# Attention's values in split passes for two heads at a time, and a new order of the linear attention's statements

## The reference

```python
x = x + L0_attn(layernorm(x))   # 16 query heads, 4 key/value heads of 128, causal softmax
x = x + L0_ffn(layernorm(x))    # 8 gated experts of 256, all computed, weighted per token by a router
x = x + L1_attn(layernorm(x))   # gated delta rule: 6 heads, short convolutions of 4 taps, gate, output projection
x = x + L1_ffn(layernorm(x))    # per sequence the 2 best of 6 gelu experts, chosen from the mean over tokens
```

```python
scores = q @ k.T ; attn = softmax(where(causal, scores, min)) ; out = attn @ v ; return out @ Wo.T + bo
```

## Time and profile before

| | us |
|---|---|
| runs | 1166.28, 1169.13, 1170.8 (median 1169.13) |
| profiled execution, its own time | 1162.17 |
| its span | 1160.4 |
| busy: TensorE, VectorE, ScalarE, GpSimd | 1098.4, 829.4, 628.2, 209.6 |
| mean granted clock of TensorE | 0.965 of full |

### The profile page before, as it was taken

One profiled execution on the slowest core, in us unless ns is written; L12 is line 12 of the kernel. 1 busy time (PEld: TensorE's weight loads), 2 busy tenths in 40 slices (PEclk: granted clock), 3 DMA queues, 4 the chain that ended last, 5 costly groups with the idle time before them and its releaser, 6 DMA issues. The chain is left out here.

```text
span 1160.4 us, 26495 instructions
## 1 busy us (share of the span) xinstructions
PE 1098.4 (95%) x9990; PEld 937.1 (81%) x9990; DVE 829.4 (71%) x2423; ACT 628.2 (54%) x1607; POOL 209.6 (18%) x246
## 2 busy tenths in 40 slices
PE   6999999999999998999999999959889999998898
PEld 4898899889988998788888889846667777777687
DVE  5777467656765785867776775798998798877454
ACT  5644444444544453544434443457877877766552
POOL 0422222222222221441000000031022102220110
PEclk9999999999999999999999999978899999997899
DMA  9200000000000000201000000011000001100323
GB/s 310 89 6 2 1 1 1 1 1 1 1 1 1 1 1 22 80 1 29 1 1 1 1 1 1 32 60 32 3 34 33 25 10 34 33 2 2 103 69 105
DMA packets 26701, 32.90 MB, mean 28 GB/s; under 512 B 4960, under 2 KB 21968, under 8 KB 26576
## 3 DMA queue, kind: packets, MB, share of 16 engines
q1 hardware_dynamic: 26576, 31.22, 8.6%
HBM read 29.04 MB, written 2.17 MB: 27 GB/s over the span
## 5 line engine op out<-in xcount | busy, mean ns | idle before, releaser
L333 DVE TENSOR_TENSOR a_ps<-a_ps,causal 128x256 f32<-128x256 f32 x128 | 54.6, 427 | 92.8 <-PE a_ps L642 92.8
L1547 PE MATMUL b_ps<-ln_high,b_high 128*128 128x512 f32 x256 | 101.2, 395 | 1.1 <-ACT gate_up_raw L1462 1.1
L692 PE MATMUL a_ps<-a_wo_high,a_oT 128*128 128x256 f32 x512 | 101.2, 282 | 0.1
L1547 PE MATMUL b_ps<-ln_low,b_high 128*128 128x512 f32 x256 | 100.4, 392 | 0.0
L1547 PE MATMUL b_ps<-ln_high,b_low 128*128 128x512 f32 x256 | 100.1, 391 | 0.0
L316 POOL TENSOR_TENSOR a_probs<-a_probs,a_inv 128x256 f32<-128x256 f32 x64 | 40.1, 627 | 330.0 <-DVE a_inv L353 330.0
L1581 PE MATMUL b_ps<-b_wd_high,b_mid 128*128 128x256 f32 x512 | 96.4, 283 | 0.0
L508 ACT CAST a_oT<-a_ps 128x512 fp32r<-128x512 f32 x64 | 37.5, 586 | 107.2 <-PE a_ps L670 107.2
L494 ACT ACTIVATE a_probs<-a_ps,a_negmax 128x128 f32<-128x128 f32 x128 | 47.1, 368 | 89.2 <-DVE a_negmax L339 76.5
L1462 ACT ACTIVATE gate_up_raw<-b_ps 128x512 f32<-128x512 f32 x64 | 37.5, 598 | 95.7 <-PE b_ps L1547 95.6
L1347 DVE TENSOR_TENSOR gate_up_raw<-gate_up_raw,b_ps 128x512 f32<-128x512 f32 x64 | 42.9, 685 | 61.9 <-ACT gate_up_raw L1462 31.9
(11 more groups left out here) (434 smaller groups left out, 3010.0 us busy)
## 6 DMA issues: line engine op xcount, KB each, us to landing
gate_up_raw<-a_scratch SPq DMA_DIRECT2D x8, 768.0 KB, 3.7
gate_up_raw<-in_D_main SPq DMA_DIRECT2D x8, 304.5 KB
x<-in_hidden SPq DMA_DIRECT2D x4, 512.0 KB, 10.7
a_raw<-in_A_q SPq DMA_DIRECT2D x4, 512.0 KB, 7.6
gate_up_raw<-in_A_o SPq DMA_DIRECT2D x1, 2048.0 KB, 13.9
gate_up_raw<-in_B_g SPq DMA_DIRECT2D x1, 2048.0 KB, 12.3
gate_up_raw<-in_B_u SPq DMA_DIRECT2D x1, 2048.0 KB, 8.4
out<-x SPq DMA_DIRECT2D x8, 256.0 KB, 3.1
```

What stands on the lines that cost most here:

```text
L333: nc.vector.tensor_tensor(diagonals, diagonals, r.causal[:].rearrange("p (o k) -> p o k", o=1).to_broadcast([P, 2, P]), ALU.add).then_inc( ...
L692: mm = nc.tensor.matmul(ps[:, out_bank(job), 0:HID], opart, wpart, start=(k == 0 and j == 0), stop=(k == QUARTER - 1 and j == len(passes) ...
L1547: mm = nc.tensor.matmul(ps[:, bank, :], wpart, xpart, start=(j == 0), stop=(j == len(passes) - 1))
```

## The change

- In attention, `values` works on two heads at once (`PAIR`), in every even step, on the two heads before it. Values and turned probabilities are split: ScalarE rounds (`take_v`, `round_pT`, the latter ahead of the step's exponentials), VectorE takes the rests (`v_rest_of`, `copy_pT`). The two heads' probabilities lie side by side, so a pass has 512 columns (256 for the second tile). `copy_oT` and `split_oT` handle a pair at a time.
- The split values and probabilities lie in the space of `gate_up_raw`'s gate weights. So only expert 2's gate weights are loaded early; the others are loaded by two DMAs when the last values are done, and ScalarE's and VectorE's users wait for them.
- In the experts' last group, convolution steps 12 and 13 come before the additions of expert pass 6 and steps 14 to 17 before those of pass 7; before, all six stood behind pass 6.
- In `delta`, the statements of the loop and of the part behind it are put in a new order on VectorE, ScalarE and TensorE. No statement is added or removed; the first part of TensorE's and VectorE's new order is in the diff.

```diff
+        EXPERT = DC * FE * WORD
+        def at(name, shape, offset):
+            return nc.alloc_sbuf_tensor_at("a_" + name, shape, F32R, offset=offset)
+        TWO_TILES = [P, GROUP_TILES // 2, NKV * HD]
+        v_highs = (at("v_high0", TWO_TILES, next_weights.raw_at + LATE_EXPERTS[-1][0] * EXPERT),
+                   at("v_high1", TWO_TILES, next_weights.raw_at + 6 * EXPERT))
...
-        pT = sb("pT", [P, 2, GROUP_BATCHES, QW])
+        PAIR = 2
+        pT_high = sb("pT_high", [P, GROUP_BATCHES, 3, PAIR, P], F32R)
+        pT_low = at("pT_low", [P, GROUP_BATCHES, 3, PAIR, P], next_weights.raw_at + LATE_EXPERTS[0][0] * EXPERT)
         WCOLS = NKV * HD
...
-                next_weights.load(sp, 0)
+                next_weights.load(sp, 0, *FIRST_EXPERT)
                 for g in range(GROUPS):
                     sp.wait_ge(r.x_loaded[g], 16)
                 sp.wait_ge(wo_split, SPLITS)
                 next_weights.load(sp, 1)
                 next_weights.load_router(sp)
+                sp.wait_ge(next_weights.loaded[0], 16)
+                sp.wait_ge(oT_ready, GROUPS * NH // PAIR)
+                for experts_of in LATE_EXPERTS:
+                    next_weights.load(sp, 0, *experts_of)
...
                     for b in range(GROUP_BATCHES):
-                        dve.wait_ge(pT_ready, 2 * G + b + 1)
-                        if G >= 2:
-                            dve.wait_ge(oT_ready, G - 1)
-                        nc.vector.tensor_copy(pT[:, G % 2, b, :], ps[:, PTB[b], 0:QW]).then_inc(pT_copied, 1)
+                        dve.wait_ge(pT_rounded, 2 * G + b + 1)
+                        if G >= PAIR:
+                            dve.wait_ge(oT_ready, G // PAIR)
+                        nc.vector.tensor_tensor(pT_low[:, b, :, G % PAIR, :], turned_bank(b),
...
+                    dve.wait_ge(v_rounded, i * GROUP_TILES + t + 1)
+                    nc.vector.tensor_tensor(v_low[t], ps[:, PROJ[t % 2], :], v_high[t].bitcast(F32), ALU.subtract
+                                            ).then_inc(v_taken, 1)
...
                     nc.vector.reciprocal(inv[:, G % 2, :], rowsum[:, G % 2, :]).then_inc(inv_ready, 1)
 
-                def split_oT(G):
-                    dve.wait_ge(oT_copied, G + 1)
-                    nc.vector.tensor_tensor(oT[:, 1, G % RING, :], ps[:, OTB[G % 2], :],
-                                            oT[:, 0, G % RING, :].bitcast(F32), ALU.subtract).then_inc(oT_split, 1)
+                def split_oT(Q):
+                    for b in range(GROUP_BATCHES):
+                        dve.wait_ge(oT_copied, GROUP_BATCHES * Q + b + 1)
+                        nc.vector.tensor_tensor(out_rows(1, Q, b), out_bank_of(b), out_rows(0, Q, b).bitcast(F32),
+                                                ALU.subtract).then_inc(oT_split, 1)
 
...
                     if h >= 1:
                         copy_pT(G - 1)
                     invert(G)
-                    if G >= 2:
-                        split_oT(G - 2)
+                    if h % PAIR and G > PAIR:
+                        split_oT(G // PAIR - 1)
+                    if h == 0:
+                        for t in range(GROUP_TILES):
...
                     if i >= 1:
-                        act.wait_ge(oT_ready, head(i, 0))
-                    nc.scalar.copy(v[t], ps[:, PROJ[t % 2], :]).then_inc(v_taken, 1)
+                        act.wait_ge(oT_ready, head(i, 0) // PAIR)
+                    nc.scalar.copy(v_high[t], ps[:, PROJ[t % 2], :]).then_inc(v_rounded, 1)
+                def round_pT(G):
+                    for b in range(GROUP_BATCHES):
+                        act.wait_ge(pT_ready, 2 * G + b + 1)
+                        if G >= PAIR:
+                            act.wait_ge(oT_ready, G // PAIR)
...
 
-                def copy_oT(G):
-                    act.wait_ge(oT_ready, G + 1)
-                    if G == 0:
+                def copy_oT(Q):
+                    act.wait_ge(oT_ready, Q + 1)
+                    if Q == 0:
                         act.wait_ge(w_split, len(BLOCKS_AT))
-                    if G >= RING:
-                        act.wait_ge(out_ready, ((G - RING) // QUARTER + 1) * GROUP_TILES)
-                    nc.scalar.copy(oT[:, 0, G % RING, :], ps[:, OTB[G % 2], :]).then_inc(oT_copied, 1)
+                    if PAIR * Q >= RING:
+                        act.wait_ge(out_ready, ((PAIR * Q - RING) // QUARTER + 1) * GROUP_TILES)
+                    for b in range(GROUP_BATCHES):
+                        nc.scalar.copy(out_rows(0, Q, b), out_bank_of(b)).then_inc(oT_copied, 1)
...
                     G = head(i, h)
+                    if h >= 1:
+                        round_pT(G - 1)
                     exps(G, 0)
                     exps(G, 1)
                     if h + 1 < NH:
                         take_q(G + 1)
-                    if G >= 1:
-                        copy_oT(G - 1)
+                    if h % PAIR == 0 and G >= PAIR:
...
                     if h == NH - 2:
                         ln_high(i, 0)
                         ln_high(i, 1)
+                    if h == NH - 1:
...
 
                 def values(i, h):
                     G = head(i, h)
+                    Q = G // PAIR
                     if h == 0:
                         pe.wait_ge(v_taken, (i + 1) * GROUP_TILES)
-                    if G < 2:
+                    if Q == 0:
                         pe.wait_ge(L["ln_taken"], DC)
-                    if G >= 2:
-                        pe.wait_ge(oT_split, G - 1)
+                    else:
+                        pe.wait_ge(oT_split, GROUP_BATCHES * Q)
                     g = slice((h // REP) * HD, (h // REP + 1) * HD)
                     for b in range(GROUP_BATCHES):
-                        pe.wait_ge(pT_copied, 2 * G + b + 1)
-                        out = ps[:, OTB[G % 2], 2 * b * P:(2 * b + 2) * P]
-                        nc.tensor.matmul(out, v[2 * b][:, g], pT[:, G % 2, b, 0:2 * P], start=True, stop=False)
-                        mm = nc.tensor.matmul(out[:, P:2 * P], v[2 * b + 1][:, g], pT[:, G % 2, b, 2 * P:QW],
-                                              start=False, stop=True)
+                        pe.wait_ge(pT_copied, 2 * (G + 1) + b + 1)
+                        turned = [x[:, b].rearrange("p s h q -> p (s h q)") for x in (pT_high, pT_low)]
+                        for t, cols, out in ((2 * b, slice(0, 4 * P), slice(0, 4 * P)),
+                                             (2 * b + 1, slice(4 * P, 6 * P), slice(2 * P, 4 * P))):
+                            passes = split_passes(v_high[t][:, g], v_low[t][:, g], turned[0][:, cols], turned[1][:, cols])
+                            for j, (vpart, ppart) in enumerate(passes):
+                                mm = nc.tensor.matmul(ps[:, OTB[b], out], vpart, ppart, start=(t == 2 * b and j == 0),
+                                                      stop=(t > 2 * b and j == len(passes) - 1))
                     mm.then_inc(oT_ready, 1)
 
...
-                    if h >= 1:
-                        values(i, h - 1)
-                    elif i >= 1:
-                        values(i - 1, NH - 1)
+                    if h and h % PAIR == 0:
+                        values(i, h - PAIR)
+                    elif h == 0 and i >= 1:
+                        values(i - 1, NH - PAIR)
...
 
-    def load(self, sp, k):
-        sp.dma_start(self.raw[:, k], self.sources[k].rearrange("e (c p) f -> p e c f", p=P)
+    def load(self, sp, k, first=0, end=NE):
+        sp.dma_start(self.raw[:, k, first:end], self.sources[k][first:end].rearrange("e (c p) f -> p e c f", p=P)
                      ).then_inc(self.loaded[k], 16)
...
+                    if k == 0:
+                        dve.wait_ge(gate_up_weights.loaded[0], 16 * (1 + len(LATE_EXPERTS)))
                     if k == 2:
...
+                            for q in range(12, 14):
+                                channels.conv(dve, 0, q)
                         if e == 7:
                             early.copy_rows(dve, ps[:, GATE[0], :], 1)
                             early.fold(dve, 1)
+                            for q in range(14, 18):
...
-                        for at_e, first in ((3, 0), (4, 6), (6, 12)):
+                        for at_e, first in ((3, 0), (4, 6)):
                             if e == at_e:
...
                     take_high(k, 0)
+                act.wait_ge(gate_up_weights.loaded[0], 16 * (1 + len(LATE_EXPERTS)))
                 take_high(0, 1)
...
-                    last(s, choose, 0)
-                    run(c, convolve, 0, 1)
                     if t == 0:
                         scan(0, 4)
                         scan(0, 5)
                         n3.newton(dve, 0, LAST_ROWS, TILES)
-                    run(c, convolve, 1, 2)
+                    last(d, pairs.add, dve, 0)
+                    last(m, statistics, 0)
                     run(m, products, 2)
                     run(m, products, 3)
```

(75 more changed lines are left out.)

250 lines of the change are left out of this document (130 added, 120 removed).

## The result

The changed kernel takes 1187.51 us (median of four runs, 1183.84 to 1193.38), the kernel before 1168.91 beside it. The ratio is 1.0174 with a 95% interval of 1.0135 to 1.0213: slower by 1.7%, and by the medians some 19 us, where I had forecast 1162 and a range up to 1177.

A forecast was written before the change was run, and what follows sets the result against it. TensorE, busy 95% of the span, was taken as the bound. Attention -4.0, experts' tail -0.9, loops 0 and last batch -2 sum to -6.9 us: 1155.3 on the profiled execution, 1162 as median forecast, range 1146 to 1177.

The forecast's parts named there:

- The passes and the chain: Attention's plain steps: a pair's value passes cost 2.08 us against 2.60; ScalarE's roundings move the chain behind them by 0.49.
- the wait: After odd attention steps, TensorE's next turning waits about 0.34 us for GpSimd, with bounds of nothing and 0.90.
- The step that failed: Attention's steps 1 and 3: a key projection of 1.4 us covers the wait, gaining 0.52 each, 3.1 in three groups.
- VectorE's lump: Odd attention steps: two heads' output split together, about 1.2 us, delays the next maxima up to 1 us, hidden by even steps.
- values' split: Attention: the values' split puts VectorE behind ScalarE before a bank is free, 0.2 us per group, 0.8 in all.
- The end of attention: Last turning to last output products: two heads' values come together behind the turning, with two copies and two splits: +1.1 us.
- Weights 0: Seven experts' gate weights, loaded behind attention's last values, arrive in time: 0 us, bounds 0 to +5.
- the tail -0.9: Experts' end: two of VectorE's six convolution steps move into its idle time before the earlier additions: -0.9 us.
- The linear attention: New order in the loops: waits and clock cancel, 0 (-15 to +12); last batch's statistics move: -2 us (0 to -3.4).
- the first rival: Attention's roundings fit ScalarE's idle time, or the reordered loops keep the clock: about 1153 us, chance 0.22.
- The third rival: Linear attention: new waits at the low tiles and the solve lengthen stretches at 1.2 GHz: 1176 us, chance 0.18.
- at 445 or 460: Sign that the forecast is wrong: attention ends at 445 or 460 us, where near 455 would show it right.

The follow-up runs named there:

- Experiment 1: Changed kernel with VectorE's output addition ahead of the split in steps 1 and 3 and behind the layer norm's second rest in step 15: 1174.91 us, ratio 1.0052.
- experiment 8: Kernel before, values' four matmuls cut to one in step 15 and, in groups 1 to 3, steps 1 and 3: 7.00, 7.10, 10.70 us for steps 1, 3, 15.
- experiment 3: Kernel before with only the changed kernel's experts' convolution steps and linear attention order, attention as before: 1163.74 us, ratio 0.9952 to the kernel before.

## Why the prediction was wrong

- **The passes and the chain: right.** A pair's passes take 2.12 (294.60 to 296.72) against my 2.08; odd and even steps take 4.84 and 7.04 against 5.1 and 6.85; the wait was mis-sized, 0.12 against 0.34, to the good. Plain pairs gain 0.26 each, where I had 0.18 to 0.20.
- **The step that failed** is "Odd steps 1 and 3 also hold a key projection of 1.4 us, which covers the wait: 0.52 each, in three groups 3.1". I asked only what covers the new wait for GpSimd, and not what the removed values covered. Product and key projection share a bank, and only these values stood between them. The term was -3.1 for steps 1 and 3; these six steps became 0.3 to 0.4 us longer each, and step 15, which stood at nothing in the sum without a reason, 3.8 to 5.3. Experiment 1 shows it (16.0 us come back when the bank is emptied first), and experiment 8 shows the cover in the kernel before.
- **VectorE's lump: right in size, wrong in place.** I had the split of two heads at 1.2 us (1.26) and weighed its lateness by the next maxima. The instruction queued directly behind it is the addition that frees the bank, and TensorE waits for that one first. My "values' split" term (+0.8 in all) was the nearest I came.
- **The end of attention: mechanism right, size off.** +1.1 forecast, +3.4 measured. I named that one head's values no longer stand before the last turning, but the 1.1 doesn't hold what that costs: the wait there is 3.60 in place of 0.60, with slow passes behind it (0.63 for two passes in place of 0.40).
- **Weights 0 and the tail -0.9: right.**
- **The linear attention: the sum right by luck, the parts not.** -2 forecast, -0.8 in the profiled execution; order and tail together -3.5 by experiment 3, where I had -2.9. The parts were +3.0 and +1.3 to 1.6 in the first two rounds, for which I had nothing, and -1.2 to -2.6 in three of the four steady ones. The -2 itself was for the last batch, whose wait of 3.41 did go, but its round is only 0.3 us shorter. Of waits a steady round keeps 1.2 us, where I had counted 1.3 to 2.0. So the first rival's case of loops that keep the clock did happen in part, and no rival of mine held the group changes. The third rival, "the loops lose clock", named a time near the measured side for a reason that experiment 3 refutes.
- **Of the signs I named**, attention's end would be "at 445 or 460" if wrong: it was 484, beyond both, because the bounds held only the wait in the chain that I had looked at. A clock under 1.00 in attention was named too, and was there.
- **The Trainium skill's page "TensorE: Matmul & The Clock Gate" (HAM oscillation)** warned that matmul bursts broken by waits fall back to the low clock. The trace agrees at the group changes (3.31 us of wait, 1.3 us of slow passes behind it). It does not for the waits of 0.12 in the plain steps, where the clock stayed at 1.00, and the page's own example has waits of several microseconds, so the prediction had stretched the rule to waits that the page doesn't speak of there.

## What to carry to other kernels

Before work is moved out of a step, list the neighbours that it stood between, and for each shared bank or buffer the instruction on another engine that must run in that time: the work's own cost is only the saving if none is there. When work is lumped, cost the lump by what stands directly behind it in its queue and who waits for that, at the irregular steps (group changes, ends) first, as those lost 29 us here and the 19 regular pairs gained 5.5. And an order written by hand is one whole from round to round: with the old list in the first round the gain of the new one was gone, and with it in the first two the kernel was slower than with either list throughout.
